# Attention scores of a graph network: place rows broadcast from DRAM and eight query banks instead of one-hots turned on TensorE, with a pipelined softmax maximum

## Reference

```
for l in range(L):
    xn = _layernorm(h, ln1_g[l], ln1_b[l])
    q = (xn @ wq[l] + bq[l]).reshape(n, H, DH)
    k = (xn @ wk[l] + bk[l]).reshape(n, H, DH)
    v = (xn @ wv[l] + bv[l]).reshape(n, H, DH)
    scores = jnp.einsum('ehd,ehd->eh', q[dst], k[src]) * scale
    m = jax.ops.segment_max(scores, dst, num_segments=n)
    ex = jnp.exp(scores - m[dst])
    z = jax.ops.segment_sum(ex, dst, num_segments=n)
    attn = ex / z[dst]
    agg = jax.ops.segment_sum(attn[:, :, None] * v[src], dst, num_segments=n)
...
```

## Time and profile before

| | us |
|---|---|
| median of 3 runs | 5814.3 (5814.27 to 5818.12) |
| the profiled execution's own time | 5781.93 |
| its span, first to last instruction | 5780.8 |
| TensorE busy | 4125.9 (71% of the span) |
| VectorE busy | 2860.4 (49%) |
| ScalarE busy | 1647.7 (29%) |
| GpSimd busy | 3686.3 (64%) |
| mean granted TensorE clock | 0.842 of full |

### The profile page before, as it was taken

One profiled execution on the slowest core, in us unless ns is written; L12 is line 12 of the kernel. 1 busy time (PEld: TensorE's weight loads), 2 busy tenths in 40 slices (PEclk: granted clock), 3 DMA queues, 4 the chain that ended last, 5 costly groups with the idle time before them and its releaser, 6 DMA issues.

```text
span 5780.8 us, 69940 instructions
## 1 busy us (share of the span) xinstructions
PE 4125.9 (71%) x19787; PEld 3148.2 (54%) x19787; DVE 2860.4 (49%) x6392; ACT 1647.7 (29%) x4900; POOL 3686.3 (64%) x3065
## 2 busy tenths in 40 slices
PE   4444443566984444379798577669999999978886
PEld 3322222344662222246566455448888888867875
DVE  6655567786544445578752566663000002134445
ACT  1111111664331111157533222222000000046664
POOL 4466667888875656688888655568878810046664
PEclk9766666999996666679898788889999999979888
DMA  8577875664227777657632555555666655546664
GB/s 263 167 242 242 256 246 158 139 161 88 25 30 230 246 247 244 174 137 167 139 34 10 134 150 151 147 114 115 154 148 138 145 153 150 153 140 177 178 176 135
DMA packets 691616, 910.55 MB, mean 158 GB/s; under 512 B 273958, under 2 KB 482901, under 8 KB 691113
## 3 DMA queue, kind: packets, MB, share of 16 engines
q0 software_dynamic: 297488, 385.75, 29.8%
q1 hardware_dynamic: 376978, 497.27, 28.7%
q10 hardware_dynamic: 16774, 23.00, 1.1%
HBM read 686.14 MB, written 219.58 MB: 157 GB/s over the span
## 4 chain that ended last, share of the span: by engine, by line
PE 45%; DVE 24%; issue 15%; another core or an unknown queue 9%; SPq 3%; DVEq 2%; ACT 1%; POOL 1%; DMA 0%; ACTq 0%; POOLq 0%
PE bank L2319 19%; PE bank L2412 6%; DVE arena L1219 5%; DVE arena L1301 4%; PE bank L2409 4%; PE bank L2224 3%; PE bank L2025 3%; PE bank L2235 3%; SPq L558 2%; DVE arena L1207 2%; DVE arena L1231 2%; DVE arena L1562 2%; DVE arena L1304 2%; PE bank L2164 1%
## 5 line engine op out<-in xcount | busy, mean ns | idle before, releaser
L815 POOL DMA_INDIRECT arena<-KVT,arena x832 | 823.0, 989 | 587.8 <-DVE arena L1304 259.6
L2319 PE MATMUL bank<-arena 128*128 128x256 f32 x5000 | 1101.1, 380 | 1.7 <-DVE arena L1619 1.2
L2319 PEld LDWEIGHTS bank<-arena 128*128 128x128 f32 x5000 | 945.0, 190 | 131.2 <-DVE arena L1619 2.0
L815 POOL DMA_INDIRECT arena<-YT,arena x416 | 404.1, 971 | 663.0 <-DMA YT<-arena 450.6
L868 POOL DMA_INDIRECT arena<-ATTR,arena x416 | 655.0, 1575 | 149.8 <-issue 149.8
L838 POOL DMA_INDIRECT sc<-arena x391 | 650.8, 1665 | 128.3 <-issue 111.9
L852 POOL DMA_INDIRECT ATT<-arena x391 | 649.5, 1661 | 124.7 <-issue 114.5
L1301 DVE TENSOR_TENSOR arena<-arena,bank 128x256 f32<-128x256 f32 x832 | 299.3, 415 | 596.5 <-remote 455.4
L2118 PE MATMUL bank<-arena 128*128 128x273 f32 x1664 | 457.4, 413 | 167.6 <-DVE arena L1348 89.1
L815 POOL DMA_INDIRECT arena<-X1T,arena x416 | 397.7, 956 | 271.3 <-DVE arena L1562 137.8
L2162 PE MATMUL bank<-arena 128*128 x832 | 299.8, 360 | 354.7 <-issue 179.7
(11 more groups left out here) (309 smaller groups left out, 6959.0 us busy)
## 6 DMA issues: line engine op xcount, KB each, us to landing
VE<-arena SPq DMA_DIRECT2D x208, 512.0 KB
arena<-VE SPq DMA_DIRECT2D x208, 512.0 KB
arena<-ATT SPq DMA_DIRECT2D x250, 320.0 KB
arena<-AM SPq DMA_DIRECT2D x250, 320.0 KB
ATT<-arena POOLq DMA_DIRECT2D x25, 1600.0 KB, 6.3
arena<-ATT SPq DMA_DIRECT2D x75, 384.0 KB
AM<-arena SPq DMA_DIRECT2D x100, 256.0 KB
arena<-KVT,arena POOLq DMA_INDIRECT x832
```

Of the source, the lines that this page charges most:

```text
L815: GP.indirect_dma_start(out=ring[:, i % n, k, :], out_offset=None, in_=table, in_offset=bass.IndirectOffsetOnAxis(ap=idx[:, 4 * i + k:4 * ...
L2319: mm = P.matmul(bank[j][:, 0:256], left[:, 128 * j:128 * (j + 1)], right[:, u, :], start=(u == 0), stop=(u == W - 1))
```

## The change

**Key loops.** locd is turned once, at the start, by four turns on TensorE and two copies on ScalarE, and written to the DRAM table LOCT as bf16, one row of 512 places for a group. In the loops SyncE reads each group's row broadcast to all 128 partitions (128 packets of 1 KB) into PLACES, a ring of six. VectorE compares it with the partition's number, which gives the turned one-hot directly in OHT; the turn on TensorE and the copy on ScalarE are gone from the loops. The queries take all eight banks. ScalarE's copy of the self edge adds the flag FL (now 0 or -1e30) as a bias, so the multiplication after the exponential goes.

**Preparation.** index_made is signalled right after isrc is made, the other places of the flags are computed from PA by a shift on TensorE (sh_1, wrap) and one comparison; the flags for the scan come straight from ScalarE's copy in B; the 26 turns back are gone; anyf and anyb are reduced in iterations 12 and 14 of k0. SyncE's share of the fetch goes from 260 of 416 chunks to 238.

**Maximum.** L1314's operation is cut in 7 pieces that feed the turns one by one; both first scans run back to back and then both carries; the turn back has 7 groups, the subtraction 14 operations, the exponential 7 pieces; ScalarE clears ACC during the scans. FB and SPs now lie in slots 1 to 7 of the value ring, so SyncE reads values from the second group on only when the turn back is done. The loads of the l3 weights in layer 1 come after four groups.

```
...
-    OHB16 = view(o_oh, 3, 512)[:, :, 0:256].bitcast(BF)
+    PLACES = view(o_oh, 6, 256).bitcast(BF)
+    LT = view(o_oh + 1152, 4, 64).bitcast(BF)
...
-    SPs, FB, BB = view(o_acc, L), view(o_acc + L, L), view(o_q, L)
+    FB, SPs, BB = view(o_big + 1024, L), view(o_big + 1024 + L, L), view(o_q, L)
...
+    LOCT = dram("LOCT", [G, 512], BF)
...
-        return (j < 2 or (j == 2 and i % 2 == 0)) if who == "sp" else (j == 3 or (j == 2 and i % 2))
+        return (j < 2 or (j == 2 and i % 7 in (0, 3))) == (who == "sp")
...
+            def load_places(i):
+                if i >= 6:
+                    SY.wait_ge(*onehot(f"k{l}", i - 5))
+                SY.dma_start(PLACES[:, i % 6, :], LOCT[i:i + 1, :].to_broadcast([128, 512])).then_inc(group_in[i % VRING].sem, 16)
...
+            for i in range(6):
+                load_places(i)
             for i in range(G):
                 SY.wait_ge(*gathered(f"k{l}", i))
                 SY.dma_start(VE[i], KV[:, i % 5, :, 256:512]).then_inc(v_kept[i % 5].sem, 16)
+                if i + 6 < G:
+                    load_places(i + 6)
...
             for i in range(G):
-                if l == 1 and i < 2:
-                    load_emb(i)
+                if i == 1:
+
+                    SY.wait_ge(*back_turned(f"w{l}", 7))
...
-        d.then(V.tensor_copy(isrc, PA[:, :, 0]))
+        V.tensor_copy(isrc, PA[:, :, 0]).then_inc(index_made.sem, 1)
...
+        V.scalar_tensor_tensor(locd, wfl, -128.0, PA[:, :, 1], ALU.mult, ALU.add).then_inc(ready.sem, 1)
+        d.then(V.tensor_tensor(FL, PA[:, :, 1], bank[5][:, 0:T], ALU.is_equal))
...
             def k_onehot(i):
+                V.wait_ge(*group_in[i % VRING](GROUP_IN[name] + i // VRING + 1))
                 if i >= 3:
-                    V.wait_ge(*onehot_mm(name, i - 2))
-                make_onehot(name, i, OHB16[:, i % 3, :], locd)
+                    V.wait_ge(*q_edge(name, 2 * (i - 2)))
+                V.tensor_scalar(OHT[:, i % 3, :], PLACES[:, i % 6, :], pcol, None, ALU.is_equal).then_inc(onehot.sem, 1)
...
-                    V.tensor_tensor(rows[:, k, :], rows[:, k, :], bank[2 + (4 * i + k) % 6][:, 0:256],
+                    V.tensor_tensor(rows[:, k, :], rows[:, k, :], bank[(4 * i + k) % 8][:, 0:256],
...
+                    if i == 12:
+                        d.mark(V.tensor_reduce(anyf, B[:, 0:L], AX, ALU.min))
+                    elif i == 14:
+                        V.wait_ge(*back_in("flags", 1))
...
-            for j in range(SB):
-                V.wait_ge(*back_turned(wn, j + 1))
...
-            V.wait_ge(*exp_made(wn, 1))
-            d.mark(V.tensor_tensor(SC[:, :, 8:16], SC[:, :, 8:16], FL.unsqueeze(2).to_broadcast([128, T, 8]), ALU.mult))
...
-            V.memset(ACC, 0.0).then_inc(acc_clear.sem, 1)
...
+            for g in range(7):
+                q, n = 4 * g, min(4, SB - 4 * g)
+                V.wait_ge(*back_turned(wn, g + 1))
+                s_ = blocked(SC)[:, q:q + n]
+                pv = bank[g % 4][:, 0:128 * n].rearrange("p (j b h) -> p j b h", b=16, h=8)
+                d.mark(V.tensor_tensor(s_[:, :, :, 0:8], s_[:, :, :, 0:8], pv, ALU.subtract))
+                V.tensor_tensor(s_[:, :, :, 8:16], s_[:, :, :, 8:16], pv, ALU.subtract).then_inc(back_read.sem, 1)
...
-            copy_onehot(name, 0)
             for i in range(G):
-                if i + 1 < G:
-                    copy_onehot(name, i + 1)
                 for k in range(4):
                     S.wait_ge(*qk(name, 4 * i + k + 1))
-                    S.activation(SC[:, 4 * i + k, 8:16], bank[2 + (4 * i + k) % 6][:, 256:264],
-                                 ACT.Copy).then_inc(self_edge.sem, 1)
+                    S.activation(SC[:, 4 * i + k, 8:16], bank[(4 * i + k) % 8][:, 256:264],
+                                 ACT.Identity, bias=FL[:, 4 * i + k:4 * i + k + 1]).then_inc(self_edge.sem, 1)
...
-            turn_onehot(name, 0, OHB16[:, 0, :], ident16)
...
-                P.wait_ge(*onehot_t(name, i + 1))
+                if l == 0 and i == 0:
+                    P.wait_ge(*back_in("flags", 1))
+                P.wait_ge(*onehot(name, i + 1))
                 for k in range(4):
-                    b_ = bank[2 + (4 * i + k) % 6]
-                    if 4 * i + k >= 6:
-                        P.wait_ge(*self_edge(name, 4 * i + k - 5))
+                    b_ = bank[(4 * i + k) % 8]
+                    if 4 * i + k >= 8:
+                        P.wait_ge(*self_edge(name, 4 * i + k - 7))
...
```

280 lines of the change are left out of this document (160 added, 120 removed).

## The result

The changed kernel takes 5728.14 us in the median of 4 runs (5717.89 to 5734.11), the kernel before 5814.28 us (4 runs, 5802.55 to 5818.12). The ratio is 0.9855, with a 95% interval of 0.9837 to 0.9874: 86 us faster, where 235 were forecast, and 8 us outside the range.

What follows compares the result with a forecast made beforehand. TensorE was taken to bound the later hops, untouched; in the key loops GpSimd waits for VectorE, with DMA the next limit. Savings of 234.6 us from 5814.3 gave 5580 us, range 5490 to 5720.

Steps and rivals of the forecast that it cites:

- The second stays, but now it is covered: Key loops: TensorE-to-VectorE hand-over of about 3 us remains, hidden by eight banks; 3.6 us a group, below GpSimd's 5.1.
- The sign that the prediction named for its own failure: Key loops: the forecast is wrong if "remote" keeps its 200 us ahead of VectorE's products.
- The pace stays: Rival, key loops: late hand-overs grow with each removed step, only 54.6 us left from other parts: 5760 us; chance 0.13.
- The broadcast: Key loops: one added DMA per group, 128 packets of 1 KB, costing the DMA engines 0.37 us a group.
- The pace of 5.53 us: Key loops: DMA is the next limit at 5.53 us a group, saving 92.7 us in k0 and 87.3 in k1.
- Fetch: Preparation: SyncE's 238 fetches at 0.81 us each and GpSimd's both end at 242 us: -17.0 us.
- Indices: Before the first gather: it waits for isrc instead of the clear at L1177, 2.8 us earlier: -2.8 us.
- Tail of k0: End of k0, last gather to maximum: VectorE two groups behind instead of four: -7.7 us.
- Maximum, layer 0: Maximum after k0: pipelined head, paired scans, exponential in pieces, clear under the scans: -23.0 us, about 57 us left.
- Layer 1: Maximum of layer 1: GpSimd's scatters hide the rest; only its wait before l1's first gather goes: -4.1 us.
- VectorE holds GpSimd up: Rival, key loops: the new one-hot's port hold slows gathers, adding up to 0.68 us a group: 5636 us; chance 0.19.

Runs made afterwards that it cites:

- e4: Changed kernel with the key-loop queries back in six banks (2 to 7) instead of eight, broadcast rows kept: 5734 us against the changed kernel's 5728.
- e11: Changed kernel with the key loops as before the change (turned one-hots, six banks), all else changed: 5730.25 us, ratio to before 0.9920.
- e8: Changed kernel with the old fetch split (260 by SyncE, 156 by GpSimd): 5257 us, ratio 0.9894 to the kernel before at 5314.91 in its series.
- e12: Changed kernel with broadcast rows loaded for two groups at a time, 64 packets of 2 KB per group: 5691.57 us against the changed kernel's 5692.11.
- e1: Changed kernel writing only 8 of 128 partitions of the value rows from group 5 on, value loops rereading five written groups: 5718 us.
- e13: Changed kernel with key-loop gathers fetching 1 KB rows instead of 2 KB from group 5 on, other rows than the reference's: 5693 us.
- e14: Changed kernel with GpSimd allowed three groups ahead of the scores instead of five: 5690 us.
- e15: Changed kernel with plain DMAs of 128 neighbouring rows replacing key-loop gathers from group 5 on, other rows: 5295.9 us, ratio to before 0.9176.
- e6: Changed kernel with GpSimd three groups ahead instead of five, in the series where the kernel before took 5314.91 us: 5258 us.
- e3: Changed kernel with two products instead of three per key-loop chunk, the lowest bf16 part of the queries left out: 5689 us.
- e2: Changed kernel with constant query windows in the key loops, so TensorE runs no register loads or operations there: 5694.5 us.

## Why the prediction was wrong

**The step that failed** is "The second stays, but now it is covered", the late hand-over of about 3 us that eight banks were to hide. It was misread in the earlier trace rows: the products that run from 2026.05 to about 2027.5 are not the ones that VectorE waits for until 2030.33. With six banks TensorE is three pairs ahead, and by count the pair that VectorE takes there is the one whose last product is this:

```profile
2015.95 0.28 PE L2164 MATMUL bank<-arena 128*128 x1
```

It ended at 2016.23 and its signal is recorded at 2030.3. So the hand-over was 14 us late, not 3, and two more banks could not cover it. The sign that the prediction named for its own failure came too: "remote" keeps 246.7 us ahead of the products. In the changed kernel's k1 it is the same (TensorE, then VectorE and GpSimd):

```profile
1949.17 0.28 PE L2225 MATMUL bank<-arena 128*128 x1 [0.47 <-issue]
...
1952.73 0.38 PE L2225 MATMUL bank<-arena 128*128 x1 [1.04 <-issue]
1957.10 0.38 PE L2223 MATMUL bank<-arena 128*128 x1 [3.99 <-issue]
...
1964.80 0.38 PE L2223 MATMUL bank<-arena 128*128 x1 [0.32 <-issue]
```

```profile
1958.48 0.75 DVE L1337 TENSOR_TENSOR arena<-arena,bank 128x256 f32<-128x256 f32 x2 [8.74 <-remote]
...
1969.08 1.41 DVE L1337 TENSOR_TENSOR arena<-arena,bank 128x256 f32<-128x256 f32 x4 [8.34 <-remote]
...
1972.02 0.94 POOL L843 DMA_INDIRECT arena<-KVT,arena  x1 [6.57 <-DVE arena L1340]
```

VectorE has its rows (SyncE passes the value halves of the next groups on at 1953.41 and 1960.73) and idles until 1958.48, for a pair whose product ended at 1946.16, and again for 8.34 us until 1969.08, for one that ended at 1948.03: 12 and 21 us late. From 1949 to 1969 TensorE itself takes 0.7, 1.4 or 4 us from one product to the next, with no engine named as the releaser. GpSimd has filled its ring at 1965.45 and goes on at 1972.02. Of TensorE's 2496 register operations ahead of its products in the two loops 441 take over 0.5 us, where 0.055 is usual; before it was 18, so the slow operations come with the change while the late signals were there already. The change does not touch what makes signals late. I took 3 us in the earlier trace rows for a fixed cost of a hand-over; VectorE's 8.75 us of idling there were nearer to the size of the thing. The rival "The pace stays" said so, with 0.13 and 5760 us; the loops gave 45 us more than it, the forecast 135 more than they did.

**What the loops gave.** 44.8 us in the first pair of traces and 51.7 in the second, as GpSimd's runs of gathers grew from mostly 16 to mostly 20 between two stops. e4 has the banks at no more than 15 us of it, e11 rows and banks together at 46.

**DMA.** The broadcast was priced at 0.37 us of DMA work for a group. q1's share went from 23.2% of 6.37 us to 31.6% of 6.17: 1.48 to 1.95 us, 0.47. The pace of 5.53 us was too high for the free condition (5.1, e8) and too low for the held one (6.2). That it came between the two is chance; its mechanism, a loop that waits for rows with DMA full, is what the free condition shows.

**Fetch.** Forecast -17.0, measured -4. I divided 210.21 us by 260 and took the 0.81 as SyncE's own price. It is 0.87 us while GpSimd fetches beside it, until 218.2, and 0.63 after that (trace of before: SyncE's first issue at 49.7 us, its 194th at 217.4, its last at 259.5); in the changed kernel it is 0.92 and 0.64. One engine's fetches get cheaper when the other has none, so work moved from one to the other is nearly neutral: e8, with the old split, has its first gather 4 us later.

**Indices.** Forecast -2.8, measured -2.8 (the first gather comes 6.73 us earlier, and VectorE's first operation on the fetched rows 3.89 earlier, at 257.61 instead of 261.50). **Tail of k0.** Forecast -7.7, measured -2.0: with VectorE held it ends as far behind as before. **Maximum, layer 0.** Forecast -23.0, measured 57.0 - 80.3 = -23.3; only the whole was measured, not its parts. **Layer 1.** Forecast -4.1, measured -5.5 and -5.9 in the two pairs of traces, with GpSimd's scatters setting l1's start, as said.

**The port.** The case "VectorE holds GpSimd up" is refuted at its own place: the 68 gathers of k1 that overlap one of the new one-hots take 0.947 us on average, the 348 others 0.945. It was the old one-hot that cost something: in k1 of before the 114 gathers that overlap L1207 take 1.050 us, the 302 others 0.946. The Trainium skill, "SBUF — State Buffer", section Who interferes with whom, would have a tensor_scalar in a two-port mode block GpSimd for the whole of it; over 104 of them nothing of that is seen in this trace (and no row tells in which mode the one-hot runs), while the earlier trace rows had shown the long copy to do it. The Trainium skill, "Perfetto Trace Analysis", section DMA Optimizations, says that DMAs below 2 KB have a significant overhead each. That is not borne out for these packets either: e12 changed packets of 1 KB for ones of 2 KB, and the share of the queue stayed.

**What stays open.** What it is in a row of indirect gathers that keeps TensorE's signals back, why TensorE's own instructions slow down in the changed kernel, and what the free condition is. Shown is that it is not the bytes (e1, e13) and not the banks (e4), that a ring of three groups does as well as one of five (e14), that the late signals are gone with plain transfers, which also come with many more stops (e15), and that the same gathers hold nobody in the free condition (e6, e8). A version that beats both kernels without giving up a part of the queries was not found; e3 beats them with two products.

## What to carry to other kernels

Where engines run ahead of each other through a ring, the instruction that a wait is for is found by count and not as the one that ended last before it: here it lay two pairs further back, and a delay of 14 us was read as 3. A stall that the trace puts to "remote" or "issue", with all inputs landed, should not be priced as a fixed step of the chain around it. Before two engines' shares of issuing are shifted, their price is to be read in stretches where both issue and where one does: an average over the whole hides that they share a resource. And where two traces come from different series, the stages that the change does not touch tell how far they can be compared.

## What the runs showed that I had not expected

- One kernel took 5772 to 5814 us in four series and 5315 in another, within 0.4% in each; two of them, 5812 and 5315, were on the same chip. The changed kernel's key loops took 637 to 648 us in the one condition; with the old fetch split they took 534 and 522 in the other.
- A signal of TensorE can arrive 17 to 21 us after its product (e2, 1950.67 to 1967.78 and 1951.35 to 1972.03) while GpSimd issues gathers in a row, and TensorE's register operations of 0.055 us can take 0.7. In the free condition every signal of the loops came 0.014 us after its product.
- A plain transfer of 128 rows of 2 KB costs GpSimd 0.54 us, the gather of as many 0.95; with plain ones the DMA share is 1.04 at 394 GB/s and a group takes 4.3 us.
- A DMA packet of 2 KB takes what two of 1 KB take (e12), so these broadcast rows are priced by bytes.
